# A four-stage attention and expert kernel on one core, with its 373 pairs of unread matmuls taken out of TensorE's queue

## The reference

```python
x = x + xattn0(_ln(x), ctx, mask)   # 16 heads of 8, masked softmax over 77 keys, projections with biases
x = x + ffn0(_ln(x))                # below
x = x + xattn1(_ln(x), ctx)         # 16 heads of 8, keys = values = ctx, only the 32 largest scores of 77
x = x + ffn1(_ln(x))                # sigmoid(xr W_r) * (relu(xk W_k)^2 W_v), with the row before mixed in

# ffn0: attention of 4 heads across the 4 sequences, then 8 experts, one per row, 256 rows at most each
y1 = ln(x + mha(x)) * g1 + b1
gates = softmax(y1 @ wg);  idx = argmax(gates);  keep = place among its expert's rows < 256
y = (y1 @ w1[idx] + b1[idx]) @ w2[idx] + b2[idx]      # no function between the two
return ln(y1 + keep * gates[idx] * y) * g2 + b2

# xattn1
top = top_k(scores, 32);  w = softmax(scores where scores >= top[-1])
```

## Time and profile before

| | before |
|---|---|
| median of 3 runs | 531.56 us (530.2 to 536.42) |
| the profiled execution, its own time | 534.36 us |
| span in its trace | 532.5 us |
| mean granted TensorE clock | 0.959 |
| busy PE, PEld | 456.8 us (86%), 335.4 us (63%) |
| busy DVE | 448.3 us (84%) |
| busy ACT, POOL | 300.8 us (56%), 309.7 us (58%) |
| matmuls | 3083, of these 746 at line 1359 |

### The profile page before, as it was taken

How to read it: one execution, slowest core, us unless ns; L and a number is a source line. 1 busy time by engine, 2 the same in 40 slices (tenths; PEclk the granted TensorE clock), 3 DMA queues, 4 the chain that set the end, 5 groups by cost and what they waited for, 6 DMA issues and landing times.

```text
span 532.5 us, 11896 instructions
## 1 busy us (share of the span) xinstructions
PE 456.8 (86%) x3083; PEld 335.4 (63%) x3083; DVE 448.3 (84%) x2970; ACT 300.8 (56%) x829; POOL 309.7 (58%) x419
## 2 busy tenths in 40 slices
PE   5779999988888888879989899988998888987686
PEld 3458986776765565656657456766666665765465
DVE  4994253967859999999999993999995999998992
ACT  2457477666254444266777666985567854154441
POOL 4574163594747747365657646876547684546721
PEclk9689999999899999999999799996999999997998
...
DMA packets 5937, 9.67 MB, mean 18 GB/s; under 512 B 744, under 2 KB 4976, under 8 KB 5616
## 3 DMA queue, kind: packets, MB, share of 16 engines
...
q10 hardware_dynamic: 288, 0.56, 0.3%
...
## 4 chain that ended last, share of the span: by engine, by line
DVE 38%; PE 33%; POOL 11%; ACT 11%; issue 6%; DMA 1%; ACTq 0%; POOLq 0%; DVEq 0%
DVE area_b L981 13%; DVE top L973 11%; PE psM L1120 5%; PE psM L1328 5%; PE psT L1359 4%; POOL dif L445 3%; PE psT L1311 2%; PE psT L1109 2%; PE psM L1275 2%; ACT mparts L626 1%; POOL prod L380 1%; DVE sc L875 1%; DVE xn L741 1%; PE psS L1090 1%; ACT p L663 1%
## 5 line engine op out<-in xcount | busy, mean ns | idle before, releaser
L1359 PE MATMUL psT<-mrow,mones 128*128 128x308 bf16 x746 | 116.9, 300 | 4.4 <-ACT vv L719 4.4
L973 DVE MAX8 top<-area_b 128x8 f32<-128x77 f32 x768 | 112.7, 229 | 0.0
L981 DVE MATCH_REPLACE8 area_b<-top,area_b 128x77 f32<-128x77 f32 x512 | 107.2, 229 | 0.0
L1359 PEld LDWEIGHTS psT<-mrow,mones 128*128 128x128 bf16 x746 | 73.5, 100 | 35.9 <-issue 13.8
L354 POOL TENSOR_TENSOR s<-s,mx 128x1232 f32<-128x1232 f32 x16 | 36.1, 2257 | 36.5 <-DVE mx L763 36.5
L981 DVE MATCH_REPLACE8 area_b<-top,area_a 128x77 f32<-128x77 f32 x256 | 53.6, 229 | 0.0
L445 POOL TENSOR_TENSOR dif<-dif,area_b 128x1232 f32<-128x1232 f32 x15 | 41.9, 2792 | 14.2 <-ACT area_b L670 14.1
L1120 PE MATMUL psM<-vblk,pT 128*128 128x135 f32 (+3 forms) x320 | 41.9, 287 | 3.2 <-DVE at L771 2.0
L981 DVE MATCH_VALUE_LOAD area_b<-top,area_b 128x8 f32 x512 | 44.0, 86 | 0.0
L1328 PE MATMUL psM<-vblk,pT 128*128 128x135 f32 (+3 forms) x320 | 41.6, 284 | 2.0 <-ACT pT L682 1.6
L433 POOL TENSOR_TENSOR dif<-area_a,top 128x1232 f32<-128x1232 f32 x16 | 36.3, 2266 | 11.0 <-ACT p L663 8.2
...
## 6 DMA issues: line engine op xcount, KB each, us to landing
...
```

The lines of the kernel that those rows point to most:

```text
L973: ins = e.max(tops[:, r, h], (left if r else scores_sb[t % RING])[:, h])
L981: ins = e.match_replace(left[:, h], tops[:, r, h], (left if r else scores_sb[t % RING])[:, h], GONE)
L1359: mm(bank[:, 0:B * KEYS], mones[:], mrow.rearrange("p b k -> p (b k)"), start=True, stop=True)
```

## The change

`FILLS` becomes 0, and all 373 `fill@` steps leave `ORDER`. The other 1825 steps stand in the same order as before, word for word, and no other line is changed. With the steps go 746 matmuls and as many weight loads, and the waits in front of them.

```diff
-FILLS = 373
+FILLS = 0
...
-tc1@2 s0@3 cc1@2 dot2@0 exp2@2 dot3@0 soft@0 fill@0 ta2@2 sc0@3 nm0@2 tb2@2 znorm@1 v1@2 mexp@0 ca2@2 cb2@2 softw@0 xbias@1
...
+tc1@2 s0@3 cc1@2 dot2@0 exp2@2 dot3@0 soft@0 ta2@2 sc0@3 nm0@2 tb2@2 znorm@1 v1@2 mexp@0 ca2@2 cb2@2 softw@0 xbias@1 wv0@0 wv1@0
...
-mark10@13 mark11@13 mark12@13 mark13@13 max20@13 max21@13 max22@13 norm@10 max23@13 acopy@10 aproduct@10 fill@248 fill@249
...
-fill@292 fill@293 fill@294 fill@295 fill@296 fill@297 fill@298 fill@299 fill@300 fill@301 fill@302 fill@303 fill@304 fill@305
-fill@306 fill@307 fill@308 fill@309 fill@310 fill@311 fill@312 fill@313 fill@314 fill@315 value@11 mark20@13 add3@10 mark21@13
...
+mark10@13 mark11@13 mark12@13 mark13@13 max20@13 max21@13 max22@13 norm@10 max23@13 acopy@10 aproduct@10 value@11 mark20@13
...
```

More of the change, by code:

```diff
@@ L1417 @@
[L1417 to L1440, removed]
@@ L1453 @@
-copy2@5 fall@6 fturn@3 keep@9 mark02@7 value@5 mark03@7 sum2@10 square2@10 max10@7 shift@3 scale2@10 max11@7 exp@6 up@3 norm@5
-max12@7 turn0@6 acopy@5 max13@7 dif@7 acts@3 mark10@7 copy0@6 down@3 norm4@4 turn1@6 mark11@7 fvalue@3 norm2@10 fturn@4 copy1@6
-mark12@7 turn@11 affine@10 shift@4 turn2@6 mark13@7 copy2@6 up@4 aproduct@5 sum3@10 half@3 max20@7 square3@10 end@3 value@6
-copy@11 max21@7 acts@4 max22@7 add3@5 store@3 max23@7 scale3@10 sum4@5 mark20@7 square4@5 down@4 scale4@5 norm3@10 moe0@11
@@ L1457 @@
-norm@6 mark21@7 acopy@6 fvalue@4 aproduct@6 norm4@5 lturn@10 mark22@7 half@4 lT@10 fturn@5 shift@5 end@4 ask@10 mark23@7
-gated0@11 up@5 add3@6 max30@7 qT@10 store@4 moe1@11 acts@5 max31@7 half@5 sum4@6 max32@7 down@5 square4@6 scores@10 max33@7
-gated1@11 scale4@6 max00@8 max01@8 keep@10 cut@7 moe2@11 max02@8 gated2@11 max03@8 norm4@6 total@11 fvalue@5 mark00@8 end@5
-drop@7 mark01@8 mark02@8 store@5 fturn@6 fall@7 sum2@11 mark03@8 square2@11 shift@6 max10@8 up@6 max11@8 scale2@11 exp@7 max12@8
@@ new lines @@
+mark02@1 yturn@3 ystore@3 mark03@1 yT@3 fall@0 max10@1 lg@3 max11@1 max12@1 max13@1 exp@0 gdiff@3 mark10@1 gexp@3 turn0@0 dif@1
+gate@3 copy0@0 mark11@1 turn1@0 copy1@0 tally@3 turn2@0 copy2@0 mark12@1 places@3 value@0 cap@3 mark13@1 max20@1 max21@1 max22@1
+turn@3 copy@3 norm@0 max23@1 acopy@0 moe0@3 aproduct@0 mark20@1 add3@0 mark21@1 gated0@3 mark22@1 sum4@0 moe1@3 square4@0
+mark23@1 scale4@0 gated1@3 max30@1 max31@1 norm4@0 max32@1 moe2@3 fturn@0 gated2@3 max33@1 shift@0 total@3 max00@2 cut@1 max01@2
@@ new lines @@
+value@1 keep@3 scale2@4 max30@2 max31@2 norm2@4 max32@2 affine@4 max33@2 turn@5 max00@3 sum3@4 cut@2 square3@4 max01@3 copy@5
+max02@3 moe0@5 max03@3 mark00@3 scale3@4 gated0@5 mark01@3 norm3@4 moe1@5 drop@2 mark02@3 lturn@4 mark03@3 lT@4 fall@2 gated1@5
+ask@4 max10@3 max11@3 qT@4 moe2@5 scores@4 max12@3 gated2@5 total@5 max13@3 keep@4 mark10@3 exp@2 mark11@3 mark12@3 turn0@2
+sum2@5 dif@3 square2@5 mark13@3 copy0@2 turn1@2 max20@3 max21@3 copy1@2 scale2@5 norm@1 turn2@2 max22@3 acopy@1 copy2@2 max23@3
@@ new lines @@
+aproduct@1 norm2@5 value@2 mark20@3 affine@5 mark21@3 add3@1 sum3@5 square3@5 mark22@3 sum4@1 turn@6 scale3@5 square4@1 mark23@3
+copy@6 scale4@1 norm3@5 moe0@6 max30@3 max31@3 norm4@1 lturn@5 max32@3 lT@5 fturn@1 gated0@6 ask@5 max33@3 max00@4 qT@5 cut@3
+moe1@6 shift@1 max01@4 max02@4 scores@5 gated1@6 max03@4 up@1 mark00@4 keep@5 moe2@6 mark01@4 gated2@6 acts@1 total@6 mark02@4
+half@1 drop@3 mark03@4 max10@4 fall@3 down@1 max11@4 sum2@6 square2@6 max12@4 fvalue@1 max13@4 norm@2 scale2@6 exp@3 mark10@4
@@ new lines @@
+affine@8 turn@9 keep@7 max32@5 max33@5 sum3@8 max00@6 cut@5 square3@8 max01@6 copy@9 moe0@9 max02@6 max03@6 gated0@9 mark00@6
+scale3@8 mark01@6 drop@5 moe1@9 mark02@6 norm3@8 fall@5 gated1@9 mark03@6 lturn@8 max10@6 lT@8 moe2@9 ask@8 max11@6 gated2@9
+qT@8 max12@6 total@9 exp@5 max13@6 mark10@6 dif@6 mark11@6 scores@8 sum2@9 mark12@6 square2@9 keep@8 mark13@6 scale2@9 max20@6
+norm2@9 max21@6 turn@10 affine@9 max22@6 copy@10 norm@3 max23@6 moe0@10 sum3@9 square3@9 mark20@6 acopy@3 scale3@9 value@4
@@ new lines @@
+gated0@10 mark21@6 aproduct@3 norm3@9 mark22@6 add3@3 sum4@3 mark23@6 square4@3 moe1@10 norm@4 scale4@3 max30@6 acopy@4 turn0@5
+max31@6 gated1@10 aproduct@4 lturn@9 max32@6 add3@4 max33@6 lT@9 moe2@10 copy0@5 ask@9 max00@7 gated2@10 cut@6 turn1@5 qT@9
+max01@7 norm4@3 total@10 copy1@5 max02@7 sum4@4 max03@7 square4@4 mark00@7 scale4@4 drop@6 turn2@5 scores@9 mark01@7 copy2@5
+fall@6 fturn@3 keep@9 mark02@7 value@5 mark03@7 sum2@10 square2@10 max10@7 shift@3 scale2@10 max11@7 exp@6 up@3 norm@5 max12@7
@@ new lines @@
+turn0@6 acopy@5 max13@7 dif@7 acts@3 mark10@7 copy0@6 down@3 norm4@4 turn1@6 mark11@7 fvalue@3 norm2@10 fturn@4 copy1@6 mark12@7
+turn@11 affine@10 shift@4 turn2@6 mark13@7 copy2@6 up@4 aproduct@5 sum3@10 half@3 max20@7 square3@10 end@3 value@6 copy@11
+max21@7 acts@4 max22@7 add3@5 store@3 max23@7 scale3@10 sum4@5 mark20@7 square4@5 down@4 scale4@5 norm3@10 moe0@11 norm@6
+mark21@7 acopy@6 fvalue@4 aproduct@6 norm4@5 lturn@10 mark22@7 half@4 lT@10 fturn@5 shift@5 end@4 ask@10 mark23@7 gated0@11 up@5
@@ new lines @@
+add3@6 max30@7 qT@10 store@4 moe1@11 acts@5 max31@7 half@5 sum4@6 max32@7 down@5 square4@6 scores@10 max33@7 gated1@11 scale4@6
+max00@8 max01@8 keep@10 cut@7 moe2@11 max02@8 gated2@11 max03@8 norm4@6 total@11 fvalue@5 mark00@8 end@5 drop@7 mark01@8
+mark02@8 store@5 fturn@6 fall@7 sum2@11 mark03@8 square2@11 shift@6 max10@8 up@6 max11@8 scale2@11 exp@7 max12@8 max13@8 turn0@7
+acts@6 mark10@8 dif@8 norm2@11 down@6 copy0@7 mark11@8 turn@12 fvalue@6 turn1@7 copy@12 mark12@8 moe0@12 copy1@7 affine@11
@@ new lines @@
+mark13@8 turn2@7 half@6 max20@8 sum3@11 end@6 square3@11 max21@8 copy2@7 max22@8 gated0@12 value@7 scale3@11 max23@8 store@6
+mark20@8 norm3@11 mark21@8 lturn@11 moe1@12 mark22@8 lT@11 mark23@8 ask@11 gated1@12 max30@8 qT@11 max31@8 moe2@12 scores@11
+gated2@12 max32@8 total@12 keep@11 max33@8 max00@9 cut@8 max01@9 max02@9 sum2@12 max03@9 square2@12 mark00@9 scale2@12 drop@8
+mark01@9 norm2@12 fall@8 mark02@9 turn@13 copy@13 mark03@9 moe0@13 max10@9 affine@12 exp@8 max11@9 max12@9 turn0@8 sum3@12
@@ L1483 @@
-copy0@10 fill@216 fturn@9 max21@11 shift@9 max22@11 turn1@10 up@9 max23@11 scale2@15 copy1@10 mark20@11 turn2@10 acts@9
-mark21@11 half@9 copy2@10 down@9 norm2@15 value@10 mark22@11 fvalue@9 affine@15 mark23@11 end@9 sum3@15 max30@11 square3@15
-max31@11 scale3@15 store@9 max32@11 max33@11 norm3@15 fill@217 fill@218 fill@219 fill@220 fill@221 lturn@15 max00@12 cut@11
-lT@15 max01@12 fill@222 ask@15 qT@15 max02@12 fill@223 fill@224 scores@15 max03@12 mark00@12 keep@15 mark01@12 drop@11 mark02@12
@@ L1487 @@
[L1487 to L1489 removed]
+add3@9 mark01@11 keep@14 half@8 moe1@15 mark02@11 fvalue@8 gated1@15 mark03@11 end@8 max10@11 drop@10 moe2@15 max11@11 store@8
@@ new lines @@
+max12@11 gated2@15 fall@10 sum4@9 max13@11 total@15 square4@9 mark10@11 mark11@11 scale4@9 exp@10 mark12@11 mark13@11 turn0@10
+sum2@15 dif@11 square2@15 max20@11 norm4@9 copy0@10 fturn@9 max21@11 shift@9 max22@11 turn1@10 up@9 max23@11 scale2@15 copy1@10
+mark20@11 turn2@10 acts@9 mark21@11 half@9 copy2@10 down@9 norm2@15 value@10 mark22@11 fvalue@9 affine@15 mark23@11 end@9
+sum3@15 max30@11 square3@15 max31@11 scale3@15 store@9 max32@11 max33@11 norm3@15 lturn@15 max00@12 cut@11 lT@15 max01@12 ask@15
@@ L1501 @@
-drop@13 end@10 norm@12 mark02@14 acopy@12 fall@13 shift@11 store@10 mark03@14 up@11 max10@14 acts@11 max11@14 aproduct@12 exp@13
-max12@14 down@11 add3@12 max13@14 half@11 turn0@13 mark10@14 sum4@12 dif@14 square4@12 mark11@14 copy0@13 fvalue@11 turn1@13
-mark12@14 copy1@13 scale4@12 mark13@14 fill@317 fill@318 turn2@13 copy2@13 max20@14 end@11 norm4@12 fill@319 fill@320 value@13
-max21@14 max22@14 store@11 max23@14 mark20@14 fturn@12 shift@12 norm@13 mark21@14 acopy@13 up@12 aproduct@13 mark22@14 add3@13
@@ new lines @@
+fturn@10 max30@13 add3@11 shift@10 max31@13 turn1@12 sum4@11 up@10 max32@13 copy1@12 max33@13 square4@11 turn2@12 acts@10
+max00@14 scale4@11 copy2@12 max01@14 down@10 value@12 cut@13 norm4@11 max02@14 fvalue@10 max03@14 mark00@14 fturn@11 mark01@14
+half@10 drop@13 end@10 norm@12 mark02@14 acopy@12 fall@13 shift@11 store@10 mark03@14 up@11 max10@14 acts@11 max11@14
+aproduct@12 exp@13 max12@14 down@11 add3@12 max13@14 half@11 turn0@13 mark10@14 sum4@12 dif@14 square4@12 mark11@14 copy0@13
+fvalue@11 turn1@13 mark12@14 copy1@13 scale4@12 mark13@14 turn2@13 copy2@13 max20@14 end@11 norm4@12 value@13 max21@14 max22@14
@@ new lines @@
+store@11 max23@14 mark20@14 fturn@12 shift@12 norm@13 mark21@14 acopy@13 up@12 aproduct@13 mark22@14 add3@13 acts@12 mark23@14
+half@12 sum4@13 down@12 square4@13 max30@14 fvalue@12 scale4@13 max31@14 max32@14 end@12 norm4@13 max33@14 fturn@13 shift@13
+max00@15 cut@14 up@13 store@12 max01@15 max02@15 acts@13 max03@15 down@13 mark00@15 half@13 fvalue@13 drop@14 end@13 mark01@15
+fall@14 mark02@15 store@13 mark03@15 max10@15 exp@14 max11@15 max12@15 max13@15 turn0@14 dif@15 mark10@15 copy0@14 mark11@15
@@ L1515 @@
```

(4 more changed lines are left out.)

117 lines of the change are left out of this document (44 added, 73 removed).

## The result

573.16 us, median of 4 runs (566.33 to 574.79), beside 530.88 us (528.17 to 536.42) of the kernel before: 1.079 times as long, 95% interval 1.0674 to 1.0907. The profiled execution took 573.08 us, its span is 571.3 us, 38.8 us more than before. Ratios, here and in the experiments, leave out as disturbed the executions that were over 1.5% slower than the fastest of their kernel; where one of four was left (the experiment without the late pairs), its four times stand in place of a ratio.

The account below looks back on a forecast made before the run. DVE sets the pace from 145 us, paying when `value` on PE comes late behind the experts' chain; 534.4 - 3 + 17 + 5 + 4 + 4 - 4 = 557.4 us, on the median's footing 555 us, range 528 to 583.

Parts of the forecast that it names:

- waits at line 1007: DVE's reciprocal waiting for `value` on PE; forecast to grow from 18.3 us to some 40.
- the tail's pieces: Pair of line 1354 and `value` pieces behind DVE's last top-32 step, forecast to run at the length of 1.2 GHz.
- the much slower rival: Half clock most of the time from 145 us on, PE the bound: 575 to 600 us, chance 0.13.
- shorter queue: PE's queue without the pairs: half of 5.6 us of chain returns, -3, ends 0 and -5.6.
- up to 225 us: 145 to 225 us: a quarter of PE's work in DVE's way, half at low clock, plus `norm@0`: +5, ends 0 and +17.
- 225 us to the end of the experts: 225 to 406 us: low clock lengthens the experts' chain (+11) and other PE work (+6): +17, ends 0 and +65.
- overlap: DVE standing before 225 us gives the experts' chain lead that it then doesn't miss: -4.
- 440 to 515 us: Each tile's weights on PE, 4.5 us, +3.6 at the low clock; `norm@13` and `norm@14` closest behind: +4, ends 0 and +7.
- tail, behind that `max`: 16 PE pieces, 7.6 us, behind DVE's last top-32 step, two thirds of +6.2: +4, ends 0 and +6.
- the low clock's share: Part of time at 1.2 GHz: a half in 145 to 225 us, a third in 225 to 406, two thirds from 500 on.
- the pairs themselves make PE late: Faster rival: without line 1359 PE can catch up and line 1007's waits return, 513 or 517 us, chance 0.05.
- No change: Clock falls more often but DVE's lead covers it: 527 to 541 us, 536 in the middle, chance 0.25.

Follow-up runs that it names:

- the experiment without the late pairs: Pairs 316 to 372 removed from the kernel before, all others kept: 547.21, 535.43, 545.30 and 546.41 us, beside 533.13 us.
- the long run: Pairs 248 to 315, 68 pairs ahead of the weights' product of tile 11, removed from the kernel before: 533.81 us, 0.9996.
- the two halves of the pairs: Kernel before with only pairs 0 to 127 kept: 556.05 us, 1.0403; with only pairs 128 to 372 kept: 553.58 us, 1.0339.
- The four kernels with added work: Kernel before with expert matmuls issued twice (550.59 us) or `up` three times (554.45); the same in the middle tiles alone (540.54, 542.42).
- the short pairs: Kernel before with all 373 pairs and their waits kept, each unread matmul 8 columns in place of 308: 572.18 us, 1.0696.

## Why the prediction was right, and where its sizes were off

The direction and the mechanism were right, and most of the marks it had named came out: mean clock 0.791 (0.75 to 0.85 forecast), nothing changed up to 145 us, the experts 16.6 us apart (16), DVE idle 26.2 us in 225 to 406 (25 to 35), 42.2 us of waits at line 1007 (some 40). Two came out in part: the clock in 225 to 406 us was 0.79 (0.8 to 0.85), and of the tail's pieces only some ran at the length of the low clock. The size was off: 573 us lies inside the stated range, but 18 us above the 555 us, over the forecast's own 542 to 570, and just under the 575 at which the much slower rival began. That the range held owes something to the room that was left for that rival. By the dates at which the two traces reach the same step the terms were (profiled execution, us):

| term | forecast | measured, and how |
|---|---|---|
| shorter queue | -3 | none seen: 533.81 beside 534.42 us without the long run; 573.16 us with no unread PE time, 572.18 with 42.6 us of it, at a low clock both |
| up to 225 us | +5 | +9.1: experts' tile 3, 225.0 to 234.1 |
| 225 us to the end of the experts | +17, less 4 for overlap | +20.7: first `max` of tile 11, 417.6 to 447.4, less 9.1 |
| 440 to 515 us | +4 | +6.4: last `max` of tile 15, 518.2 to 554.4, less 29.8 |
| tail, behind that `max` | +4 | +2.6: span 532.5 to 571.3, less 36.2 |
| sum | +23 | +38.8 |

Three terms were mis-sized. First the low clock's share: "for 225 to 406, which is denser, a third" is 0.42 (a mean of 0.79), the half for 145 to 225 is 0.58 (0.71), and two thirds for the tail 0.74 (0.63 from 533 us on; behind the last `max`, from 554.4 us, it is 0.60 by a mean of 0.70). With these in the prediction's own formulas the terms are 10 x (4.7 + 2.5) x (0.42 - 0.09) = 23.8, 10.7 x 0.81 x 0.58 + 1 = 6.0, 7.2 x 0.58 - 1 = 3.2 and 6.2 x 0.74 = 4.6, in all 37.6 where 38.8 was measured. Second the overlap of -4: the two halves of the pairs add up to the whole within 1.5 us and give no sign of it, though with their intervals they don't rule it out. Third the -3 for the shorter queue.

That the formula meets the sum is in part luck: its terms miss the table's by 2 to 3 us each, up and down. It counted ten tiles for 225 to 406 us, where the trace has the first expert matmuls of twelve (3 to 14, the last at 398.03 us); with twelve its term would have been +18 in place of +17. And it took PE's work on the experts' chain in full and the rest by half. The four kernels with added work give 0.64, 0.73, 0.62 and 0.74 us of time for one us of PE (17.4 / 27, 21.3 / 29, 7.4 / 12, 9.3 / 12.6), on the chain and off it, each uncertain by 0.1 to 0.3. By that, the 118 us of needed PE work in 225 to 406, 0.81 x 0.33 longer, are 31.5 us of PE time, and 20 to 23 us of the span: near the 20.7, from another account. Over the whole kernel it comes out lower: PE's needed work took 413.9 us in place of 339.9 (456.8 less 116.9), and the span grew by 38.8, 0.52 for one. I had read the experts' chain as the place of the loss; the runs speak for all of PE's needed work, whose steps stand in one order, with `value` behind all of them. The unread pairs, where they stand, are not part of that: 42.6 us of short ones cost nothing that can be seen.

The rivals: "the pairs themselves make PE late" falls with the run of 68 (0.9996) and with the short pairs (1.0696). "No change" would have needed DVE's lead to cover the low clock; taking out either half of the pairs already costs 3 to 4%. The figure of under 1% by which the Trainium skill ("TensorE: Matmul & The Clock Gate", section "What's actually happening") supported it is one for warming up. It is no measure for this kernel, in which the clock falls again and again: 7.9%. "Much slower" had the right step in it, more cold time than I took, and its lower end was missed by 2 us only; but PE was not busy all of the time (72%), and the clock was above 0.5 in every stretch.

Not tried: the waits ahead of the pairs taken away with the pairs left in.
